# Turning attention's queries, keys and probabilities by VectorE's square blocks and device memory instead of TensorE transposes

## The chip, the cores and the metric

The kernel runs on one core of a Trainium2 chip. The metric is the device time of one execution in microseconds (us). The engines of the core run side by side and meet only at semaphores: TensorE (PE) multiplies matrices, VectorE (DVE), ScalarE (ACT) and GpSimd (POOL) work element by element, and SyncE (SP) issues nearly all transfers (DMA).

## What is computed

The reference is a block of two layers on 16 sequences of 64 tokens of width 512, all in float32. The part that matters here is the first one, a cross-attention with 32 query heads and 8 key heads:

```
kv = concatenate([context, latents], axis=1)             # 128 keys for each sequence
q = rms_norm(latents @ Wq)   per head, 32 heads of 128
k = rms_norm(kv @ Wk)        per head, 8 heads of 128;   v = kv @ Wv
scores = einsum('bhgqd,bhkd->bhgqk', q, k) * 128 ** -0.5
probs = softmax(scores);     out = (probs @ v) @ Wo
```

A feed-forward layer with 4-bit weights follows, then a second attention and a second feed-forward layer with low-rank additions. The change doesn't touch those three, but the 4-bit weights are unpacked (dequantized) by VectorE in the background of the first attention.

## The kernel before, in words

The first attention is cut into 64 units: 8 key heads times 8 pairs of sequences (`UNITS`). A unit has four query heads for two sequences of 64 tokens, so its queries are a tile of 128 tokens by 4 x 128 (`b_q`), its keys and values two tiles of 128 by 128 each (`b_kv`), its scores four tiles of 128 by 128 (`b_s`). Products that need float32 accuracy are three passes over a high and a low part (`HI`, `LO`; `PASSES`): ScalarE copies a value to its rounded high part, another engine subtracts to get the low part.

The work is software-pipelined by hand. Each engine has a function for one step `j` (`pe_step0`, `act_step0`, `dve_step0`, `pool_step0`), and in a step it treats several units at once, each in another phase: `st.has(lag, UNITS)` is the part for unit `j - lag`. Each engine runs its instructions strictly in the order in which the code writes them; a wait on a semaphore holds all that is behind it on that engine.

In a step TensorE does, in order: the query projection of unit `j` (12 matmuls, L354), the transposes of queries and keys of unit `j-1` (six, L380 and L383, from `qn` and `kn`), the key and value projection of `j` (24, L366), the scores of `j-1` (L394), the transposes of the probabilities of `j-2` (four, L406), the output product of `j-3` (12, L418) and the product of probabilities and values of `j-2` (6, L431).

The queries and keys need a normalization first: ScalarE squares (L527, L542), VectorE sums (L579, L589), GpSimd takes the power -1/2 (L671, L674), VectorE multiplies (L585, L609). The softmax is VectorE's maximum (L595), ScalarE's four exponentials, each with a sum (L553), VectorE's reciprocal and multiplication (L614, L616).

In the background of the steps: the next key head's weights are loaded (`weight_load`), rounded by ScalarE at the end of its step (`hi_piece`, L455 or L459), and their low part computed by GpSimd at the end of its step (`lo_piece`, L468 or L472). In steps 5 to 57, 35 chunks of 4-bit weights are unpacked in three VectorE operations each (`dequant`, L1062, L1066, L1069), two in a step, in two fixed places of VectorE's order (`dve_between`); their factors are gathered by GpSimd (`gather_row`, L849), the chunks loaded and stored by SyncE (L776, L785, L788).

## Time and profile before

| what | value |
|---|---|
| time, median of 3 runs | 1143.39 us (1141.55 to 1143.66) |
| the profiled execution's own time | 1142.94 us, of which the span of its instructions 1141.1 us |
| busy share of the span | TensorE 96%, VectorE 68%, ScalarE 46%, GpSimd 35% |
| granted TensorE clock | 0.99 of full speed, mean |
| transfers | 89.05 MB, 78 GB/s over the span |

The span is that of one execution recorded by the profiler; around it lie 1.8 us. The first attention takes the part of the span up to about 760 us. A step's length can be read from the start of the same matmul in two steps that follow each other: the scores (L394) of one begin at 400.10 us and of the next at 411.18 us, so a step takes 11.08 us.

### The profile page before, as it was taken

The page shows a single profiled execution, that of the slowest core. Times are in us where ns is not written, and L with a number is a line of the kernel's source. Part 1 is how long each engine was busy: PE and PEld are TensorE (multiplying, and loading weights), DVE is VectorE, ACT ScalarE, POOL GpSimd, SP SyncE. Part 2 cuts the span into 40 slices and gives each one's busy share as a digit, 9 for nine tenths or more (in the row PEclk, how much of TensorE's full clock was granted, in tenths as well). Part 3 has the DMA queues.
Part 4 walks back from the last instruction along what each step waited for, and adds up shares of the span by engine and source line. Part 5 has one row for each costly group of instructions (what it writes and reads, how often), then busy time and mean ns, then how long its engine had stood idle before and what let it go on. Part 6 is the DMA issues. An engine that isn't in the chain of part 4 may idle for free. (4 is left out here: it accounts for less than half of the span.)

```text
span 1141.1 us, 18735 instructions
## 1 busy us (share of the span) xinstructions
PE 1097.6 (96%) x6533; PEld 950.9 (83%) x6533; DVE 773.4 (68%) x1496; ACT 523.9 (46%) x1398; POOL 398.5 (35%) x385
## 2 busy tenths in 40 slices
PE   4899999999999999999999999999999999888998
PEld 3789899998989999898989989878877777677877
DVE  7577777777777777777777765764344566889863
ACT  4354544545455454544544444443223445465531
POOL 4443343433334343343434321210002334575521
PEclk7899999999999999999999999999999999999999
DMA  6322323332332323233232120022202244143300
GB/s 221 82 79 71 104 63 98 88 96 69 92 103 64 97 89 96 68 102 106 70 103 84 50 91 1 1 80 89 65 1 56 65 111 111 43 104 77 84 10 37
DMA packets 65376, 89.05 MB, mean 78 GB/s; under 512 B 15544, under 2 KB 35024, under 8 KB 65284
## 3 DMA queue, kind: packets, MB, share of 16 engines
q1 hardware_dynamic: 60788, 70.95, 22.0%
q0 software_dynamic: 4496, 16.91, 4.8%
q8 instruction: 53, 0.87, 0.3%
q14 instruction: 39, 0.32, 0.1%
HBM read 64.64 MB, written 10.74 MB: 66 GB/s over the span
## 5 line engine op out<-in xcount | busy, mean ns | idle before, releaser
L366 PE MATMUL bank<-wqkv,kvT 128*128 128x256 f32 x1536 | 199.9, 286 | 2.1 <-DVE vv L570 2.1
L418 PE MATMUL bank<-wo,aoT 128*128 128x512 f32 x768 | 191.8, 398 | 0.0
L366 PEld LDWEIGHTS bank<-wqkv,kvT 128*128 128x128 f32 x1536 | 187.9, 191 | 3.7 <-DVE vv L570 3.6
L354 PE MATMUL bank<-wqkv,kvT 128*128 128x512 f32 x768 | 189.1, 395 | 1.6 <-DVE qn L585 1.6
L354 PEld LDWEIGHTS bank<-wqkv,kvT 128*128 128x128 f32 x768 | 141.8, 191 | 28.9 <-issue 1.8
L418 PEld LDWEIGHTS bank<-wo,aoT 128*128 128x128 f32 x768 | 139.6, 188 | 27.2
L671 POOL TENSOR_TENSOR rms<-msq,half_neg 128x4 f32<-128x4 f32 x64 | 80.0, 1249 | 202.7 <-DVE msq L581 202.5
L527 ACT ACTIVATE qsq<-bank 128x512 f32<-128x512 f32 x64 | 38.2, 597 | 115.3 <-PE bank L354 115.3
L553 ACT ACTIVATE prob<-bank,nmax 128x128 f32<-128x128 f32 x256 | 90.1, 371 | 2.2 <-DVE nmax L595 2.2
L585 DVE TENSOR_TENSOR qn<-bank,rms 128x512 f32<-128x512 f32 x64 | 44.3, 692 | 61.0 <-POOL rms L671 61.0
L674 POOL TENSOR_TENSOR rms<-msq,half_neg 128x2 f32<-128x2 f32 x64 | 44.8, 699 | 116.5 <-DVE msq L591 116.5
L542 ACT ACTIVATE ksq<-bank 128x256 f32<-128x256 f32 x64 | 24.5, 383 | 125.8 <-PE bank L366 125.8
L903 PE MATMUL bank<-x2T,wgu 128*128 128x512 f32 (+1 forms) x336 | 81.0, 396 | 1.0 <-issue 0.6
L579 DVE TENSOR_REDUCE ssq<-qsq 128x4 f32<-128x512 f32 x64 | 44.0, 687 | 49.0 <-ACT qsq L527 48.2
L903 PEld LDWEIGHTS bank<-x2T,wgu 128*128 128x128 f32 (+1 forms) x336 | 62.2, 186 | 16.9 <-DVE wd L864 0.8
L1975 POOL TENSOR_TENSOR pr<-pr,rc 128x512 f32<-128x512 f32 x52 | 54.4, 1049 | 54.7 <-DVE rc L1839 54.6
L394 PE MATMUL bank<-kT,qT 128*128 128x128 f32 x512 | 67.6, 275 | 1.2 <-ACT qT L531 1.2
L514 ACT ACTIVATE aoT<-bank 128x512 fp32r<-128x512 f32 x64 | 38.3, 599 | 59.6 <-PE bank L431 59.6
L920 PE MATMUL bank<-wd,hT 128*128 128x512 f32 (+1 forms) x264 | 65.5, 395 | 0.0
L547 ACT ACTIVATE pT<-bank 128x512 fp32r<-128x512 f32 x64 | 38.2, 597 | 58.7 <-PE bank L406 58.7
L394 PEld LDWEIGHTS bank<-kT,qT 128*128 128x128 f32 x512 | 62.8, 192 | 1.4 <-ACT qT L531 1.4
L468 POOL TENSOR_TENSOR wqkv<-wqkv_raw,wqkv 128x768 fp32r<-128x768 f32 x28 | 51.6, 1844 | 31.4 <-ACT wqkv L455 31.1
(176 smaller groups left out, 2131.1 us busy)
## 6 DMA issues: line engine op xcount, KB each, us to landing
wqkv_raw<-in_L_xattn_Wq_dram SPq DMA_DIRECT2D x32, 256.0 KB, 2.6
wo_raw<-in_L_xattn_Wo_dram SPq DMA_DIRECT2D x32, 256.0 KB, 2.8
qS<-qhl SPq DMA_DIRECT2D x32, 256.0 KB, 3.8
wload<-w_gu SPq DMA_DIRECT2D x20, 256.0 KB, 3.2
w_gu<-qch SPq DMA_DIRECT2D x16, 256.0 KB, 2.3
kS<-chl SPq DMA_DIRECT2D x32, 128.0 KB, 3.1
qch<-_L_ffn_down_qweight_dram SPq DMA_DIRECT2D x10, 256.0 KB, 3.6
w_d<-qch SPq DMA_DIRECT2D x10, 256.0 KB, 2.0
```

The lines of the kernel that those rows point to most:

```text
L354: mm = pe.matmul(b_q[:, :], kvT[:, l, kt, p, 1:3, :], wqkv[:, par, r, kt, 0:QW], start=(kt == 0 and n == 0), stop=(kt == KT - 1 and n == 2))
L366: mm = pe.matmul(b_kv[:, b * 256:(b + 1) * 256], kvT[:, l, kt, p, 2 * b:2 * b + 2, :], wqkv[:, par, r, kt, QW:QKV], start=(kt == 0 and n = ...
L394: mm = pe.matmul(b_s[:, n * P:(n + 1) * P], qT[:, b, 2 * hp:2 * hp + 2, :], kT[:, b, :], start=True, stop=True)
L418: mm = pe.matmul(b_o[:, :], aoT[:, l, h, :, :], wo[:, par, r, h, :], start=(h == 0 and n == 0), stop=(h == G - 1 and n == 2))
L468: pool.tensor_tensor(wqkv[:, par, LO, n, :], wqkv_raw[:, n % 2, :], wqkv[:, par, HI, n, :].bitcast(F32), ALU.subtract).then_inc(s_wqkv, 1)
L553: act.activation(prob[:, n, :], b_s[:, n * P:(n + 1) * P], ACT.Exp, bias=nmax[:, n:n + 1], accum_out=psum_row[:, n:n + 1]).then_inc(s_exp, 1)
L585: dve.tensor_tensor(qn[:, :, :], b_q[:, :].rearrange("p (h d) -> p h d", h=G), rms[:, 0:4].unsqueeze(2).to_broadcast([P, G, HD]), ALU.mult ...
L671: pool.tensor_tensor(rms[:, 0:4], msq[:, 0:4], half_neg[:, 0:4], ALU.pow).then_inc(s_rq, 1)
L674: pool.tensor_tensor(rms[:, 4:6], msq[:, 4:6], half_neg[:, 4:6], ALU.pow).then_inc(s_rk, 1)
L903: mm = pe.matmul(b[0:w, :], wgu[:, f, l, m, kt, 0:w], x2T[:, r, kt, :], start=(kt == 0 and k == 0), stop=(kt == KT - 1 and k == 2))
L920: mm = pe.matmul(f_d[t][:, :], hT[0:w, l, t * P:(t + 1) * P], wd[0:w, f, r, :], start=(f == 0 and k == 0), stop=(f == FT - 1 and k == 2))
L1975: pool.tensor_tensor(of[:, to + t % KT, :], of[:, to + t % KT, :], rc1[:, t % 4:t % 4 + 1].to_broadcast([P, D]), ALU.mult).then_inc(s_n1, 1)
```

## The change

TensorE no longer transposes anything in these steps. A tile of 128 by 128 is turned in two halves. VectorE transposes it in square blocks of 32 by 32 (`dve.transpose`), after a multiplication that it did before too, which now writes to a PSUM bank (`b_n`) in an order of elements that suits the blocks. Then SyncE stores the result to device memory (`blocks_out`: 128 rows of 2 KB, for keys 1 KB) and loads it back in another order (`blocks_back`: each row of SBUF from four pieces of 512 bytes, for keys 256 bytes), which puts the blocks in their places. So each unit has six transfers more: queries, keys and probabilities, out and back.

With it come these: ScalarE sums the squares itself, in four plus two smaller operations, in place of VectorE's two sums; the key's scale is applied by ScalarE after the load; the probabilities' low part is subtracted by GpSimd from SBUF instead of by VectorE from PSUM; the values bank `b_kv` is doubled. The scores of unit `j-1` now stand at the end of TensorE's step, behind the output product, the maximum and the exponentials come a step later, and the product with the values is that of unit `j-3`, behind the query projection. In the tables: the load of the first three weight tiles of the feed-forward layer moves into steps 62 to 64.

```diff
+            def sp_step0(st):
+                if st.has(1, UNITS):
+                    sp.wait_ge(s_k_out, st.done(1, 16))
+                    wait(sp, s_s, st.done(2))
+                    blocks_back(sp, kT[:, :, :, :], k_turn).then_inc(s_k_back, 16)
+                if st.has(2, UNITS):
+                    sp.wait_ge(s_pB, st.done(2))
+                    wait(sp, s_p_back, st.done(3, 16))
+                    blocks_out(sp, p_turn, pB[:, :, :, :]).then_inc(s_p_out, 16)
+                if st.j >= 1:
+                    weight_load(st.j - 1)
+                sp_stores(sp, st.j)
...
+                if st.has(2, UNITS):
+                    sp.wait_ge(s_p_out, st.done(2, 16))
+                    wait(sp, s_pv, st.done(3))
+                    blocks_back(sp, pT[:, LO, :, :, :].bitcast(F32), p_turn).then_inc(s_p_back, 16)
+                if st.has(0, UNITS):
+                    sp.wait_ge(s_qB, st.done(0))
+                    wait(sp, s_q_back, st.done(1, 16))
+                    blocks_out(sp, q_turn, qB[:, :, :, :]).then_inc(s_q_out, 16)
+                sp_loads(sp, st.j)
+                if st.has(0, UNITS):
+                    sp.wait_ge(s_kB, st.done(0))
+                    wait(sp, s_k_back, st.done(1, 16))
+                    blocks_out(sp, k_turn, kB[:, :, :, :]).then_inc(s_k_out, 16)
+                    sp.wait_ge(s_q_out, st.done(0, 16))
+                    wait(sp, s_s, st.done(1))
+                    blocks_back(sp, qT[:, :, :, :], q_turn).then_inc(s_q_back, 16)
...
+        def blocks_out(sp, to, frm):
+            return sp.dma_start(to.rearrange("a p r -> (a p r)").rearrange("(p c) -> p c", p=P),
+                                frm.rearrange("p b h t -> p (b h t)"))
+
+        def blocks_back(sp, to, frm):
+            return sp.dma_start(to.rearrange("p a h t -> p a (h t)"), frm.rearrange("a p r -> p a r"))
...
         def act_step0(st):
             act = nc.scalar
+            if st.has(2, UNITS):
+                act.wait_ge(s_max, st.done(2))
...
+                    act.activation(prob[:, n, :], b_s[:, n * P:(n + 1) * P], ACT.Exp, bias=nmax[:, n:n + 1],
+                                   accum_out=psum_row[:, n:n + 1]).then_inc(s_exp, 1)
+            if st.has(0, UNITS):
+                act.wait_ge(s_q, st.done(0))
...
+                for h in range(G):
+                    act.activation(b_sq[:, h * HD:(h + 1) * HD], b_q[:, h * HD:(h + 1) * HD], ACT.Square,
+                                   accum_out=ssq[:, h:h + 1]).then_inc(s_qsq, 1)
...
             if st.has(2, UNITS):
-                act.wait_ge(s_pt, st.done(2))
+                act.wait_ge(s_p_back, st.done(2, 16))
                 wait(act, s_pv, st.done(3))
-                act.activation(pT[:, HI, :, :], b_pt[:, :].rearrange("p (b q) -> p b q", b=2), ACT.Copy).then_inc(s_phi, 1)
...
+                act.activation(pT[:, HI, :, :, :], pT[:, LO, :, :, :].bitcast(F32), ACT.Copy).then_inc(s_phi, 1)
             hi_piece(act, st)
 
         def dve_step0(st):
             dve = nc.vector
+            if st.has(2, UNITS):
+                dve.wait_ge(s_s, st.done(2))
+                wait(dve, s_exp, st.done(3, 4))
+                dve.tensor_reduce(nmax[:, :], b_s[:, :].rearrange("p (n k) -> p n k", n=4), AX, ALU.max,
+                                  negate=True).then_inc(s_max, 1)
+            dve_between(dve, st.j, "exp")
+            if st.has(2, UNITS):
+                dve.wait_ge(s_exp, st.done(2, 4))
+                dve.reciprocal(rsum[:, :], psum_row[:, :]).then_inc(s_rec, 1)
+                dve.wait_ge(s_rec, st.done(2))
+                dve.tensor_tensor(b_n[:, :].rearrange("p (b a k) -> p b a k", b=4, a=4),
+                                  prob[:, :, :].rearrange("p a (k b) -> p b a k", b=4),
+                                  rsum[:, :].unsqueeze(1).unsqueeze(3).to_broadcast([P, 4, 4, 32]),
+                                  ALU.mult).then_inc(s_pn, 1)
+                dve.wait_ge(s_pn, st.done(2))
+                wait(dve, s_p_out, st.done(3, 16))
+                dve.transpose(pB[:, :, :, :].rearrange("p b h t -> p (b h t)"), b_n[:, :]).then_inc(s_pB, 1)
...
+            if st.has(2, UNITS):
+                pool.wait_ge(s_phi, st.done(2))
+                pool.tensor_tensor(pT[:, LO, :, :, :], pT[:, LO, :, :, :].bitcast(F32), pT[:, HI, :, :, :].bitcast(F32),
+                                   ALU.subtract).then_inc(s_plo, 1)
             gather_row(pool, st.j)
             lo_piece(pool, st)
```

The two sets of rows that follow are TensorE's order in one step of the middle of the attention, before and after. `bank0` holds the queries, `bank4` the scores, `bank5` the turned probabilities, `bank6` the product with the values, `bank7` the output product.

```order
255 L354 MATMUL bank0<-wqkv,kvT 128x512 x12
256 L380 MATMUL bank2<-ident,qn 128x128 x4
257 L383 MATMUL bank3<-ident,kn 128x128 x2
258 L366 MATMUL bank1<-wqkv,kvT 128x256 x24
259 L394 MATMUL bank4<-kT,qT 128x128 x4
260 L406 MATMUL bank5<-ident,prob 128x128 x4
261 L418 MATMUL bank7<-wo,aoT 128x512 x12
```

```order
215 L400 MATMUL bank0<-wqkv,kvT 128x512 x12
216 L442 MATMUL bank6<-pT,vv 128x256 x6
217 L418 MATMUL bank1<-wqkv,kvT 128x256 x24
218 L465 MATMUL bank7<-wo,aoT 128x512 x12
219 L428 MATMUL bank4<-kT,qT 128x128 x4
```

The ten transposes (L380, L383, L406) are gone, the scores stand behind the output product, and the product with the values (L431 before, L442 after) stands behind the query projection.

SyncE's queue in the same part of the program, before and after: names with `_turn` are the tensors in device memory through which a tile is turned.

```order
129 L258 DMA wqkv_raw<-in_L0_xattn_Wq_dram 128x512
130 L259 DMA wqkv_raw<-in_L0_xattn_Wk_dram 128x128
131 L260 DMA wqkv_raw<-in_L0_xattn_Wv_dram 128x128
132 L788 DMA w_gu<-qch 128x4x128
133 L264 DMA wo_raw<-in_L0_xattn_Wo_dram 128x512
```

```order
251 L339 DMA p_turn<-pB 128x512
252 L265 DMA wqkv_raw<-in_L0_xattn_Wq_dram 128x512
253 L266 DMA wqkv_raw<-in_L0_xattn_Wk_dram 128x128
254 L267 DMA wqkv_raw<-in_L0_xattn_Wv_dram 128x128
255 L833 DMA w_gu<-qch 128x4x128
256 L343 DMA pT<-p_turn 128x4x128
257 L339 DMA q_turn<-qB 128x512
258 L821 DMA qch<-in_L0_ffn_up_qweight_dram 128x1x512
259 L339 DMA k_turn<-kB 128x256
260 L343 DMA qT<-q_turn 128x4x128
261 L343 DMA kT<-k_turn 128x4x64
```

The load of the turned probabilities (`pT<-p_turn`) stands behind up to five other issues: the three of a weight piece and the one or two of a store.

GpSimd's order in a step, before and after (`pT` is the low part of the probabilities, `wo` or `wqkv` the low part of a weight piece):

```order
138 L671 TENSOR_TENSOR rms<-msq,half_neg 128x4
139 L674 TENSOR_TENSOR rms<-msq,half_neg 128x2
140 L849 DMA rows<-table_up_1,idx 128x1024
141 L472 TENSOR_TENSOR wo<-wo_raw,wo 128x512
```

```order
153 L712 TENSOR_TENSOR rms<-msq,half_neg 128x4
154 L715 TENSOR_TENSOR rms<-msq,half_neg 128x2
155 L718 TENSOR_TENSOR pT<-pT 128x512
156 L904 DMA rows<-table_up_2,idx 128x704
157 L506 TENSOR_TENSOR wqkv<-wqkv_raw,wqkv 128x768
```

One operation of 512 elements is added, ahead of the gather and the weight piece.

## Rows read from the trace of the kernel before

**Rows 1.** Busy us (and instructions) of PE, PEld, DVE, ACT, POOL; clock, DMA share, GB/s.

```profile
88.42:675.66 587.24, 587.24 (x3807) 530.90 (x3806) 427.39 (x792) 286.71 (x847) 223.56 (x191) 1.00 0.27 84
737.21:759.97 22.76, 20.97 (x118) 17.77 (x117) 17.71 (x34) 12.56 (x28) 6.21 (x7) 1.00 0.11 35
```

**Rows 2.** Waits of TensorE, 60 to 700 us: total us, times, longest.

```profile
PE bank L366 <- DVE vv L570: 0.4, 1, 0.4
```

**Rows 3.** Timeline of TensorE, 404 to 416 us: start, length, engine, line.

```profile
404.90 2.91 PE L354 MATMUL bank<-wqkv,kvT 128*128 128x512 f32 x12
407.65 0.60 PE L380 MATMUL bank<-ident,qn 128*128 128x128 f32 x4
408.09 0.38 PE L383 MATMUL bank<-ident,kn 128*128 128x128 f32 x2
408.22 3.12 PE L366 MATMUL bank<-wqkv,kvT 128*128 128x256 f32 x24
411.18 1.06 PE L394 MATMUL bank<-kT,qT 128*128 128x128 f32 x8
412.07 0.60 PE L406 MATMUL bank<-ident,prob 128*128 128x128 f32 x4
412.43 3.00 PE L418 MATMUL bank<-wo,aoT 128*128 128x512 f32 x12
415.27 0.88 PE L431 MATMUL bank<-pT,vv 128*128 128x256 f32 x6
```

**Rows 4.** Timeline of the softmax and the work behind it, 402 to 406 us.

```profile
402.12 0.36 ACT L553 ACTIVATE prob<-bank,nmax 128x128 f32<-128x128 f32 x1
...
403.49 0.65 ACT L459 ACTIVATE wo<-wo_raw 128x512 fp32r<-128x512 f32 x1
403.65 0.18 DVE L614 RECIPROCAL rsum<-psum_row 128x4 f32<-128x4 f32 x1 [0.37 <-ACT prob L553]
403.87 0.69 DVE L616 TENSOR_TENSOR prob<-prob,rsum 128x512 f32<-128x512 f32 x1
...
404.23 1.48 POOL L472 TENSOR_TENSOR wo<-wo_raw,wo 128x512 fp32r<-128x512 f32 x1 [0.91 <-ACT wo L459]
404.48 1.52 DVE L1062 TENSOR_SCALAR qch<-qch,shift 128x512 int32<-128x512 int32 x1
```

**Rows 5.** DMA issues on the page: count, KB each, median us from issue to landing.

```profile
wo_raw<-in_L_xattn_Wo_dram SPq DMA_DIRECT2D x32, 256.0 KB, 2.8
...
wload<-w_gu SPq DMA_DIRECT2D x20, 256.0 KB, 3.2
w_gu<-qch SPq DMA_DIRECT2D x16, 256.0 KB, 2.3
...
w_d<-qch SPq DMA_DIRECT2D x10, 256.0 KB, 2.0
```

**Rows 6.** Landings of the store L788, 100 to 700 us.

```profile
DMA to landing us min/median/max: 1.9/2.3/4.0
```

**Rows 7.** One line's durations: ACT L455, DVE L1062 (ns min/median/max).

```profile
L455 ACT ACTIVATE wqkv<-wqkv_raw x28: 835/865/866, 39.5 to 636.8; 128x768 fp32r<-128x768 f32 x28
...
L1062 DVE TENSOR_SCALAR qch<-qch,shift x35: 397/487/2102, 87.3 to 653.7; 128x512 int32<-128x512 int32 x26, 128x352 int32<-128x352 int32 x8, 96x512 int32<-96x512 int32 x1
```

**Rows 8.** Timeline of SyncE's queue: start, length of the issue.

```profile
431.99 0.38 SPq L788 DMA_DIRECT2D w_gu<-qch  x1
```

**Rows 9.** DMA queue q1, 398.6:401.6 (L788 alone) and 498.7:502 (L785 alone): packets, MB, share.

```profile
q1 hardware_dynamic: 528, 0.26, 30.0%
...
q1 hardware_dynamic: 144, 0.26, 21.0%
```

**Rows 10.** Timeline, 409 to 411 us: GpSimd's power beside VectorE's unpacking.

```profile
409.28 0.69 DVE L1066 TENSOR_TENSOR qch<-qch,rows 128x512 f32<-128x512 int32 x1
409.45 1.42 POOL L671 TENSOR_TENSOR rms<-msq,half_neg 128x4 f32<-128x4 f32 x1 [3.74 <-DVE msq L581]
410.90 0.69 DVE L585 TENSOR_TENSOR qn<-bank,rms 128x512 f32<-128x512 f32 x1 [0.93 <-POOL rms L671]
```

273 lines of the change are left out of this document (127 added, 146 removed).

## The prediction

> **What bounds the kernel now.** I read the busy time by stretch first. Over 587 us, which are steps 5 to 57 of the attention (53 steps of 11.08 us), TensorE is busy in every microsecond at full clock, while VectorE is busy for 427 us, ScalarE 287 and GpSimd 224, and the transfers take 27% of the DMA engines [rows 1]. The list of waits agrees: in 640 us TensorE waited once, for 0.4 us [rows 2]. So in a step the length is the sum of what TensorE issues. The timeline divides it by the starts of its groups: query projection 2.75 us, transposes of queries and keys 0.57, key projection 2.96, scores 0.89, transposes of probabilities 0.36, output product 2.84, and the product with the values, up to the next step's start at 415.98 us (404.90 + 11.08), 0.71 [rows 3].
>
> **What goes from TensorE.** The ten transposes: 0.57 + 0.36 = 0.93 us of a step. If nothing else bound, a step would be 10.15 us, and 64 steps would save 60 us. The question is what the new paths allow in 10.15 us, since each engine holds its order.
>
> **The path of the probabilities.** It is a ring: the exponentials of one unit, their turning, the load, then on ScalarE the high part and a weight piece, and behind these the exponentials of the next unit. What can't run faster than this ring sets the step. From one start of the exponentials to the next:
> - exponentials up to the reciprocal: 403.65 - 402.12 = 1.53 us; reciprocal to multiplication 0.22; multiplication 0.69 + 0.04 for the semaphore [rows 4].
> - The block transpose of 512 elements: no row shows one. From below it is 0; from above I take twice an operation of that size, 1.4 us. I take 0.69, the duration of the multiplication of the same size, the nearest row [rows 4].
> - The store of 256 KB: 2.0 us for rows of 2 KB, 2.3 for pieces of 512 bytes [rows 5]. I take 2.15. The worst of that second kind took 4.0 [rows 6].
> - The load in pieces of 512 bytes: between 2.8 (rows of 2 KB) and 3.2 (from a tensor that was itself stored by this program) [rows 5]; I take 2.95. Three semaphores around the two transfers: 0.15.
> - High part from SBUF 0.65, like L459 [rows 4], less the 0.05 by which it overlaps its successor; weight piece 0.65 or 0.87 in turn [rows 4, 7], mean 0.76, of which I count 0.74.
>
> Sum: 1.53 + 0.22 + 0.73 + 0.69 + 2.15 + 2.95 + 0.15 + 0.60 + 0.74 = 9.76 us. That is under 10.15, with 0.4 us of room. Two things use more than the room.
>
> *Issue and queueing.* Between store and load SyncE issues a weight piece and, in 35 of 53 steps, a store of unpacked weights, up to five issues of about 0.4 us [rows 8], 2.0 us behind the 0.4 of the store itself, so that the load can be issued a few tenths late; and their 256 to 640 KB lie in the queue ahead of the load. A 256 KB store in 512-byte pieces fills all engines for 0.30 x 3.0 = 0.90 us, one in 2 KB rows for 0.21 x 3.3 = 0.69 [rows 9]. The six new transfers are 1.25 MB in a step and by these prices 4.0 to 4.5 us of all DMA engines, so their share goes from 27% to about 67%. I put queueing at 0.45 us of the ring, between 0 (all falls into gaps) and 1.6 (the store at 3.0, the load at 3.7).
>
> *VectorE and GpSimd.* The rows show that these two stop each other on operands in SBUF: the unpacking L1062 takes 0.49 us as a rule but up to 2.10 [rows 7]; in the timeline it took 1.52 where it began 0.25 us after GpSimd's L472, and ended 0.29 us after that did [rows 4]. The other way round GpSimd's power took 1.42 us where it began beside an unpacking [rows 10]. Before, the multiplication L616 mostly ran while GpSimd was idle. Now GpSimd subtracts the low part of 512 elements (1.48, like L472) just as ScalarE goes on to the weight piece, then issues a gather, then does its own weight piece (1.48 to 1.84); that lies over the time 0.7 to 3.5 us behind the start of the exponentials, and the multiplication stands at 1.75. A stall is between 0 and 1.2 us; I take 0.6.
>
> The Trainium skill has this rule on its page SBUF — State Buffer, section Who interferes with whom: a VectorE instruction with two SBUF inputs and a GpSimd instruction that reads SBUF exclude each other, and who starts first keeps the port for the whole instruction. The trace agrees for the unpacking; no row shows it for L616. By that rule alone, with GpSimd always first, the stall would be 1.2 us in each step.
>
> So the ring is 9.76 + 0.45 + 0.6 = 10.8 us in steps 5 to 57.
>
> **VectorE's own ring.** The transposes (512, 512, 256 elements) replace two sums (512, 256) and the low part of 512, so its busy time stays 427.39 / 587.24 x 11.08 = 8.06 us. But it now waits through the exponentials (1.7 us from the maximum's end, with one unpacking of about 0.6 inside them), and for the two powers, of which the first alone cost it 0.93 us before [rows 10]; now the low parts of output and values, about 1.0 us, lie beside the first and an unpacking beside the second, so I take 0.6 for both. That is 8.06 - 0.6 + 1.7 + 0.6 = 9.8 us, 10.4 with the stall of 0.6: close behind the ring of the probabilities. ScalarE, 286.71 / 587.24 x 11.08 = 5.4 us busy, gets about 0.5 us more and has room.
>
> What hides the rest: the queries' round trip of about 5.3 us starts some 7.5 us into a step and is needed 9.3 us into the next; that of the keys starts 2 us later and its load is scaled by ScalarE about 5 us into the next step. Without this cover each would cost its whole 5.3 us.
>
> **The sum.** Steps 5 to 57: 53 x (10.8 - 11.08) = -15 us. The other 11 steps have no unpacking: about -0.93 each, less for the first ones, which fill the pipeline, and the last, which have the next layer's statistics on VectorE: -7. The end: before, from 737.21 us, 22.76 us were left to the last output product, and TensorE was busy for 20.97 of them [rows 1]. After, two units' exponentials must pass the ring one behind the other: 9.8, then 3.2 + 5.3 + 0.6 to the second one's high part, 1.5 for its low part, then values, their parts and the output product, 0.7 + 1.5 + 2.9, and 1 ahead of it: 26.5, so +4. The start I leave at nothing; its one more round trip is behind the second query projection. -15 - 7 + 4 = -18 us. The profiled execution took 1142.94 us, 0.45 under the median of the runs shown; so 1125 us.
>
> **Rivals.**
> - *All is hidden.* If the stall and queueing fall in the 0.4 us of room, TensorE bounds again: 64 x -0.93 + 4 = -56, so 1087 us. For it: both terms are zero from below, and the sum has 0.4 us. Against: the DMA share of 67%, and GpSimd's new operation stands just there.
> - *The round trip is too long (slower).* The place is the wait of ScalarE for the probabilities' load. Without its trip the ring is 9.76 - 5.25 = 4.5 us, 5.1 with the stall, so it passes 11.08 when store and load together take over 6.0 us, where I forecast 5.7. With the store at 2.6, the load at 3.7 and 0.3 of late issue, it is 6.6, the step 11.7: 53 x 0.62 - 3 = +30, so 1173 us. For it: store maxima of 4.0 [rows 6] at 27% share, and the share more than doubles.
> - *VectorE's new operations are dear.* With block transposes at twice the row's price its ring is 10.4 + 0.69 + 0.69 + 0.41 = 12.2 us: 53 x 1.1 + 4 = +62, some 1205 us. The Trainium skill, page Advanced Engine Details and Errata, section SBUF Cachelines, speaks for it: reads that touch another 16-byte line each time pay a penalty, and the multiplication now reads every fourth float32. No run here shows such a read.
>
> **Numbers.** Forecast as above (1100 to 1141 us) 0.39; all hidden 0.19; round trip too long 0.28; dear operations 0.08; a step within a few hundredths of 11.08, no change, 0.06. Faster by over 0.2%, which is about what a measurement of this kernel tells from none, is 0.58, slower 0.36. The range reaches from the first rival to the middle of the second: 1086 to 1176 us.
>
> **What would show it.** Right: scores of two steps 10.8 us apart; TensorE idle a few tenths in a step, ended by ScalarE's or VectorE's low part of the output, by the low part of the probabilities or by `qn`; ScalarE idle ahead of the high part (L591), ended by the DMA; the multiplication L606 often over 0.69 us. STREAM_TRANSPOSE at about 0.69, stores at 2.0 to 2.4, loads at 2.8 to 3.3. Wrong: landings over 3.5 us, or a transpose over 1 us (slower), or TensorE without idle time and 10.15 us steps (all hidden).

## The result, and the profile after

The changed kernel takes 1220.26 us (median of 4 runs, 1217.82 to 1222.04) beside 1142.71 for the kernel before (4 runs in the same session): a ratio of 1.0673, interval 1.0653 to 1.0693, so 77.5 us slower. The forecast was 1125 us, the range 1086 to 1176. The profiled execution took 1221.74 us, 78.8 more than that of before.

The busy time of the stretch that answers to [rows 1], 52 spacings of the multiplication L606 (steps 5 to 57), in the same columns, and under it that of the drain of the attention:

```profile
92.64:722.27 629.63, 545.80 (x3214) 467.07 (x3213) 456.33 (x780) 289.13 (x1296) 289.44 (x242) 1.00 0.62 187
760.00:840.00 80.00, 60.10 (x300) 50.69 (x298) 43.30 (x89) 29.06 (x108) 20.44 (x22) 0.87 0.34 108
```

A step takes 629.63 / 52 = 12.11 us in place of 11.08, and TensorE, which was never idle, is busy for 87% of it. No other engine is over 73%. No engine is full, so what sets the step is a chain of waits. The list of TensorE's waits, 87 to 690 us, against the one wait of 0.4 us in [rows 2]:

```profile
PE bank L442 <- POOL pT L718: 41.9, 45, 3.2
PE bank L465 <- DVE aoT L622: 35.1, 34, 1.5
PE bank L465 <- issue: 6.8, 6, 1.6
```

The page's costliest groups and its DMA issues say where the chain is: ScalarE is idle for 319 us ahead of the high part of the probabilities L591, always for the load, and the multiplication takes 2131 ns on average where [rows 4] had 0.69 us.

```profile
L591 ACT ACTIVATE pT<-pT 128x512 fp32r<-128x512 f32 x64 | 40.5, 632 | 319.3 <-DMA pT<-p_turn 319.3
L606 DVE TENSOR_TENSOR bank<-prob,rsum 128x512 f32<-128x512 f32 x64 | 136.4, 2131 | 2.2
...
q_turn<-qB SPq DMA_DIRECT2D x64, 256.0 KB, 4.0
...
p_turn<-pB SPq DMA_DIRECT2D x64, 256.0 KB, 2.0
pT<-p_turn SPq DMA_DIRECT2D x64, 256.0 KB, 3.9
```

One turn of the ring in the timeline, from the first exponential of a unit (L554) to that of the next, which answers to [rows 4]:

```profile
406.54 0.35 ACT L554 ACTIVATE prob<-bank,nmax 128x128 f32<-128x128 f32 x1
...
407.40 1.02 POOL L904 DMA_INDIRECT rows<-table_up,idx  x1 [0.17 <-issue]
...
408.06 0.18 DVE L604 RECIPROCAL rsum<-psum_row 128x4 f32<-128x4 f32 x1 [3.21 <-ACT prob L554]
408.27 2.94 DVE L606 TENSOR_TENSOR bank<-prob,rsum 128x512 f32<-128x512 f32 x1
408.46 1.86 POOL L506 TENSOR_TENSOR wqkv<-wqkv_raw,wqkv 128x768 fp32r<-128x768 f32 x1
411.24 0.72 DVE L612 STREAM_TRANSPOSE pB<-bank 128x512 f32<-128x512 f32 x1
411.99 0.33 SPq L339 DMA_DIRECT2D p_turn<-pB  x1
...
414.05 0.38 SPq L343 DMA_DIRECT2D pT<-p_turn  x1
...
418.08 0.63 ACT L591 ACTIVATE pT<-pT 128x512 fp32r<-128x512 f32 x1 [6.19 <-DMA pT<-p_turn]
...
419.14 0.35 ACT L554 ACTIVATE prob<-bank,nmax 128x128 f32<-128x128 f32 x1
```

The multiplication began at 408.27 and ended at 411.21, 0.89 us after GpSimd's weight piece L506 (410.32), although the piece began 0.19 us later than it did. Of the 50 multiplications between 90 and 700 us in the trace, 49 end 0.88 to 0.91 us after the piece beside them: they are 1.32 to 1.77 us long in the 17 where the piece stands alone and had begun 0.4 to 1.1 us earlier, and 2.60 to 3.37 in the 32 where a gather stands ahead of the piece, which then begins 0.18 to 0.62 us later than they do.

Where the time was lost can be read from the starts of the output products (L418 before, L465 after):

| output product of unit | before | after | later by |
|---|---|---|---|
| 2 | 90.41 | 96.14 | 5.7 |
| 56 | 690.06 | 745.97 | 55.9 |
| 60 | 734.38 | 789.65 | 55.3 |
| 63 | 757.08 | 834.42 | 77.3 |
| end of the span | 1141.1 | 1219.9 | 78.8 |

So 50 us are the steps, 22 the last three units, 6 the start, and what follows the attention costs 1.5. The four units from 56 to 60 win only 0.6: three of these steps take 10.0 to 10.1 us, the fourth 13.6.

### The profile page after: what moved, and what is told of

It is laid out like the page before. It is cut to its first block and busy times, and to the rows that moved or that the text cites. A ratio compares the mean times of both kernels' runs of the same rounds, so it can differ in the third digit from the quotient of the medians.

```text
span 1219.9 us, 18668 instructions
## 1 busy us (share of the span) xinstructions
PE 1065.9 (87%) x5893; PEld 893.0 (73%) x5893; DVE 810.7 (66%) x1496; ACT 535.9 (44%) x1974; POOL 478.7 (39%) x449
## 5 line engine op out<-in xcount | busy, mean ns | idle before, releaser
L465 PE MATMUL bank<-wo,aoT 128*128 128x512 f32 x768 | 193.7, 401 | 53.5 <-DVE aoT L622 46.7
L465 PEld LDWEIGHTS bank<-wo,aoT 128*128 128x128 f32 x768 | 141.2, 190 | 90.4 <-DVE aoT L622 54.3
L418 PE MATMUL bank<-wqkv,kvT 128*128 128x256 f32 x1536 | 198.8, 287 | 0.0
L400 PE MATMUL bank<-wqkv,kvT 128*128 128x512 f32 x768 | 195.2, 403 | 1.7 <-DVE bank L631 1.7
L418 PEld LDWEIGHTS bank<-wqkv,kvT 128*128 128x128 f32 x1536 | 193.2, 196 | 0.2
L591 ACT ACTIVATE pT<-pT 128x512 fp32r<-128x512 f32 x64 | 40.5, 632 | 319.3 <-DMA pT<-p_turn 319.3
L718 POOL TENSOR_TENSOR pT<-pT 128x512 fp32r<-128x512 f32 x64 | 84.4, 1319 | 204.1 <-ACT pT L591 204.1
L606 DVE TENSOR_TENSOR bank<-prob,rsum 128x512 f32<-128x512 f32 x64 | 136.4, 2131 | 2.2
L712 POOL TENSOR_TENSOR rms<-msq,half_neg 128x4 f32<-128x4 f32 x64 | 65.6, 1025 | 116.0 <-DVE msq L619 115.7
L442 PE MATMUL bank<-pT,vv 128*128 128x256 f32 x384 | 62.9, 300 | 54.7 <-POOL pT L718 54.5
L442 PEld LDWEIGHTS bank<-pT,vv 128*128 128x128 f32 x384 | 50.4, 191 | 79.2 <-POOL pT L718 78.8
L604 DVE RECIPROCAL rsum<-psum_row 128x4 f32<-128x4 f32 x64 | 11.4, 178 | 141.7 <-ACT prob L554 141.7
L715 POOL TENSOR_TENSOR rms<-msq,half_neg 128x2 f32<-128x2 f32 x64 | 59.2, 924 | 110.3 <-DVE msq L640 110.3
L554 ACT ACTIVATE prob<-bank,nmax 128x128 f32<-128x128 f32 x256 | 89.6, 360 | 7.7 <-DVE nmax L599 7.7
L562 ACT ACTIVATE bank<-bank 128x128 f32<-128x128 f32 x256 | 70.9, 277 | 2.1 <-PE bank L400 2.1
```

The source lines that it names most:

```text
L400: mm = pe.matmul(b_q[:, :], kvT[:, l, kt, p, 1:3, :], wqkv[:, par, r, kt, 0:QW], start=(kt == 0 and n == 0), stop=(kt == KT - 1 and n == 2))
L418: mm = pe.matmul(kv_bank(st, 0)[:, b * 256:(b + 1) * 256], kvT[:, l, kt, p, 2 * b:2 * b + 2, :], wqkv[:, par, r, kt, QW:QKV], start=(kt == ...
L442: mm = pe.matmul(b_pv[:, b * 256:(b + 1) * 256], vv[:, par, l, b, :], pT[:, r, :, b, :], start=(n == 0), stop=(n == 2))
L465: mm = pe.matmul(b_o[:, :], aoT[:, l, h, :, :], wo[:, par, r, h, :], start=(h == 0 and n == 0), stop=(h == G - 1 and n == 2))
L554: act.activation(prob[:, n, :], b_s[:, n * P:(n + 1) * P], ACT.Exp, bias=nmax[:, n:n + 1], accum_out=psum_row[:, n:n + 1]).then_inc(s_exp, 1)
L562: act.activation(b_sq[:, h * HD:(h + 1) * HD], b_q[:, h * HD:(h + 1) * HD], ACT.Square, accum_out=ssq[:, h:h + 1]).then_inc(s_qsq, 1)
```

## The experiments

Each time stands beside runs of the kernel before in its own session. For the ring I read the same five stretches out of each timeline, as means over 52 turns (units 3 to 55, which are steps 5 to 57); they add up to the spacing of the multiplications. The forecast's row has its terms in the same stretches (0.73 + 0.6; 0.69; 2.15 + 0.10; 2.95 + 0.45 + 0.05; 0.60 + 0.74 + 1.53 + 0.22). "Rest" is conversion L591 to the next multiplication: conversion, weight piece, exponentials, reciprocal.

| kernel | time, us | step | multiply | its end to store issue | store issue to load issue | load issue to conversion | rest |
|---|---|---|---|---|---|---|---|
| forecast | 1125 | 10.8 | 1.33 | 0.69 | 2.25 | 3.45 | 3.09 |
| changed | 1220.3 | 12.11 | 2.35 | 0.78 | 2.25 | 3.84 | 2.89 |
| e1 prob in PSUM | 1163.4 | 11.10 | 0.70 | 0.78 | 3.05 | 3.69 | 2.89 |
| e2 read in a row | 1202.3 | 11.76 | 2.00 | 0.78 | 2.30 | 3.81 | 2.89 |
| e3 load first | 1267.0 | 13.03 | 2.54 | 2.06 | 2.35 | 3.19 | 2.90 |
| e5 queue | 1208.1 | 11.93 | 2.46 | 0.79 | 2.53 | 3.25 | 2.91 |
| e6 rows of 2 KB | 1203.0 | 11.79 | 2.33 | 0.78 | 2.24 | 3.54 | 2.89 |
| e11 e1 and e5 | 1200.0 | 11.64 | 0.70 | 0.89 | 3.89 | 3.23 | 2.93 |
| e12 GpSimd later | 1299.4 | 13.56 | 1.10 | 0.78 | 4.75 | 4.04 | 2.88 |
| e13 e12, loads later | 1238.9 | 12.48 | 1.10 | 0.78 | 2.24 | 5.38 | 2.98 |
| e15 piece later | 1176.5 | 11.26 | 1.11 | 0.78 | 2.80 | 3.68 | 2.88 |

**e1: the exponentials kept in PSUM.**

```diff
-                    act.activation(prob[:, n, :], b_s[:, n * P:(n + 1) * P], ACT.Exp, ...
+                    act.activation(b_s[:, n * P:(n + 1) * P], b_s[:, n * P:(n + 1) * P], ACT.Exp, ...
-                                  prob[:, :, :].rearrange("p a (k b) -> p b a k", b=4),
+                                  b_s[:, :].rearrange("p (a k b) -> p b a k", a=4, b=4),
```

> Exponentials are written over the scores in PSUM bank 4, and the multiply behind the reciprocal reads them there, so that it has no large operand in SBUF; the next scores wait for the multiply. Exclusion theory (the multiply is held up by GpSimd's elementwise operations and gather over SBUF, and its 2.6 us set the ring): the multiply falls to 0.70 to 1.1 us with or without GpSimd at work, the spacing of the multiplies in steps 5 to 57 falls from 12.1 us to 10.4 to 10.8, the kernel to 1140 to 1160 us. Rival (the transfers set the ring; VectorE's delay only fills time in which the load would be waited for): the multiply shortens, but the load lands later or is waited for longer, the spacing stays above 11.7, the kernel above 1195 us.

1163.44 us, ratio 1.0173 (1.0151 to 1.0195). All multiplications take the same time (ns, min/median/max):

```profile
L606 DVE TENSOR_TENSOR bank<-bank,rsum x64: 698/699/700, 56.5 to 768.7; 128x512 f32<-128x512 f32 x64
```

The spacing, 11.10 us, misses the exclusion theory's window of 10.4 to 10.8, and so does the time by 3 us, since of the 1.65 us won 0.80 come back in the store:

```profile
409.33 0.37 SPq L343 DMA_DIRECT2D kT<-k_turn  x1
411.52 0.33 SPq L339 DMA_DIRECT2D p_turn<-pB  x1
```

The keys' load is now issued 2.2 us ahead of the store of the probabilities, where it was 4.7 in the changed kernel (407.31 and 411.99); the store takes 3.0 us in the median, not 2.0. That this load is what makes it longer is a reading of the timeline and not shown: in 18 turns of e1 the load was issued 3 to 4 us ahead, and the store took 3.2 us there too. The rival is out, since it had the spacing above 11.7.

**e2: the same multiplication, reading one float32 after another.** Its probabilities end up in another order, so the output isn't the reference's; sizes and counts are the same.

```diff
-                                  prob[:, :, :].rearrange("p a (k b) -> p b a k", b=4),
+                                  prob[:, :, :].rearrange("p a (b k) -> p b a k", b=4),
```

> The multiply reads the probabilities one float32 after another, not every fourth: same count, same result tile, the elements stand in another order (the attention output is that of a permuted key order). If the strided read has a price of its own of 0.4 us (1.09 against 0.69 us alone) and the rest is GpSimd's exclusion: 0.70 us where GpSimd is idle, still 2.2 to 2.9 us beside its operations, the kernel 1200 to 1216 us. Rival (the strided read is what makes it 2.6 us): the median falls below 1.2 us, the kernel to 1140 to 1160 us.

1202.31 us, ratio 1.0518 (1.0494 to 1.0542). The shortest one takes 0.70 us against 1.07, the median 2.27 against 2.61:

```profile
L606 DVE TENSOR_TENSOR bank<-prob,rsum x64: 699/2271/2946, 58.2 to 800.3; 128x512 f32<-128x512 f32 x64
```

So reading every fourth float32 costs 0.35 to 0.4 us, and the rest of the excess isn't the stride. Shortest, median and time are the first theory's.

**e3 and e5: SyncE's order.** e3 puts weight loads and the stores and tile loads of the feed-forward weights behind the load of the probabilities and the store of the queries.

```diff
-                if st.j >= 1:
-                    weight_load(st.j - 1)
-                sp_stores(sp, st.j)
...
                     blocks_out(sp, q_turn, qB[:, :, :, :]).then_inc(s_q_out, 16)
+                if st.j >= 1:
+                    weight_load(st.j - 1)
+                sp_stores(sp, st.j)
```

> In each step SP issues the load of the turned probabilities and the store of the queries ahead of the weight loads, the w_gu and w_d stores and the tile loads, which before stood between the store and the load of the probabilities. If the load's 4.0 us (3.2 in the quiet steps 58 to 61) come from standing behind those transfers: the landing falls to 3.2 to 3.4 us, the step by 0.6 to 0.7, the kernel to 1180 to 1190 us. Rival (it shares the rings with whatever runs at the time, 63% busy): the landing stays at 3.8 to 4.1, the kernel within 8 us of 1220.

1266.96 us, ratio 1.1078 (1.1058 to 1.1098): 47 us slower than the changed kernel, which neither theory had. The load did land in 3.2 us, but SyncE's queue shows what was put behind what:

```profile
416.43 0.43 SPq L833 DMA_DIRECT2D w_gu<-qch  x1
420.14 0.55 SPq L821 DMA_DIRECT2D qch<-in_L_ffn_up_qweight_dram  x1
420.79 0.53 SPq L339 DMA_DIRECT2D k_turn<-kB  x1
```

The load of quantized rows waits for the landing of the store issued at 416.43, and the keys' store stands behind it: 8.9 us after the store of the probabilities (411.91), where in the changed kernel it was 4.6 us (411.99 and 416.63). e5 gives that load to the next step, behind the keys' load, and puts the weight transfers behind the keys' store.

```diff
+                if st.j >= 1:
+                    sp_loads(sp, st.j - 1)
                 if st.has(2, UNITS):
                     sp.wait_ge(s_pB, st.done(2))
...
                     blocks_out(sp, k_turn, kB[:, :, :, :]).then_inc(s_k_out, 16)
+                if st.j >= 1:
+                    weight_load(st.j - 1)
+                sp_stores(sp, st.j)
```

> SP's order changed without the fault of the run before: the weight loads and the w_gu and w_d stores stand behind the store of the keys, and the loads of quantized rows, which wait for those stores, go to the next step behind the load of the keys. Nothing but turning transfers is issued between the store and the load of the probabilities. Queue theory: that load lands in 3.2 to 3.4 us as in the run before, nothing is held behind the quantized load, the step falls by 0.5 to 0.8 us to 11.3 to 11.6, the kernel to 1180 to 1195 us. Rival (the rings' total load makes the 4.0 us, and the last run's 3.2 us was only its longer step): the landing stays at 3.7 to 4.0, the kernel 1205 to 1225 us.

1208.11 us, ratio 1.0569 (1.0551 to 1.0586). The load's share fell by 0.6 us as the queue theory said, and 0.3 of it came back in the store, since keys and queries are now loaded later and lie beside it. The step fell by 0.18, so the gain is the rival's, though its reason isn't.

**e6: the load in rows of 2 KB**, in place of pieces of 512 bytes. The probabilities end up in the wrong places, so the output isn't the reference's; the bytes are the same.

```diff
-                    blocks_back(sp, pT[:, LO, :, :, :].bitcast(F32), p_turn).then_inc(s_p_back, 16)
+                    rows_back(sp, pT[:, LO, :, :, :].bitcast(F32), p_turn).then_inc(s_p_back, 16)
```

> The load of the turned probabilities fetches one row of 2 KB for each partition in place of four pieces of 512 bytes (the same 256 KB, elements in the wrong places, so the output is of mixed probabilities). If the pieces are what makes the load slower than the store (4.0 against 2.0 us): it lands in 2.0 to 2.6 us, the step falls by 1.4 to 1.9 until another ring or TensorE sets it, the kernel 1130 to 1150 us. Rival (it is the other transfers in flight): 3.5 to 4.0 us, the kernel above 1195 us.

1202.97 us, ratio 1.0529 (1.0512 to 1.0547): the rival's window. The piece size is worth 0.3 us of the load, the transfers issued ahead of it 0.6 (e5). The changed kernel shows the second by itself: from the load's issue to the conversion it is 3.3 us in the median of the 18 turns with no store of unpacked weights between store and load, 4.1 in the 34 with one.

**e12, e13, e15: GpSimd's order**, operands as in the changed kernel. e12 moves gather and weight piece one step later, behind the power of the queries.

```diff
                 pool.tensor_tensor(rms[:, 0:4], msq[:, 0:4], half_neg[:, 0:4], ALU.pow).then_inc(s_rq, 1)
+            if st.j >= 1:
+                gather_row(pool, st.j - 1)
+                lo_piece(pool, Step(0, st.j - 1))
...
-            gather_row(pool, st.j)
-            lo_piece(pool, st)
```

> The changed kernel with one thing moved: GpSimd's gather and its weight piece, which ran beside the multiply, stand one step later behind the power of the queries, when the multiply and the block transpose behind it are over; operands and their places in memory are as in the changed kernel. Exclusion theory (the multiply waits out GpSimd's operations): it takes 1.1 to 1.5 us (its own price, and what is left of GpSimd's low part of the probabilities), the spacing in steps 5 to 57 falls to 10.8 to 11.3 us, the kernel to 1150 to 1180 us. Rival (reading every fourth float32 from SBUF is slow whenever DMA and other engines are at work, and GpSimd only looks like the cause): it stays above 2 us, the kernel above 1205 us.

1299.43 us, ratio 1.1357 (1.1337 to 1.1377). The multiplication takes 1.10 us, the exclusion theory's number, and yet the kernel is the slowest of all. The store's row tells why:

```profile
414.65 0.33 SPq L339 DMA_DIRECT2D p_turn<-pB  x1
418.30 0.34 SPq L271 DMA_DIRECT2D wo_raw<-in_L_xattn_Wo_dram  x1
418.74 0.53 SPq L343 DMA_DIRECT2D pT<-p_turn  x1
```

The weight load waits until GpSimd's piece has freed its buffer, and the load of the probabilities stands behind it in the queue. e13 issues the weight loads a step later as well (`weight_load(st.j - 2)`).

> The changed kernel with GpSimd's gather and weight piece one step later, behind the power of the queries, and SP's weight loads one step later as well, so that they find their buffer free and nothing waits in SP's queue. Exclusion theory: the multiply takes 1.1 us as in the last such run, 1.5 us less than in the changed kernel, the store 2.0 and the load 4.0 us as there, the spacing 10.6 to 11.3 us, the kernel 1145 to 1180 us. Rival (the exclusion only moves to another of VectorE's operations on the ring, as to the powers or the keys' multiply): the multiply is short but the spacing stays at 11.8 us or more, the kernel above 1200 us.

1238.85 us, ratio 1.0837 (1.0809 to 1.0865), step 12.48: in the rival's window, but not for the rival's reason. Now it is the load that takes 5.4 us on average, beside the gather's transfers:

```profile
407.82 0.45 SPq L343 DMA_DIRECT2D pT<-p_turn  x1
...
411.85 0.63 ACT L591 ACTIVATE pT<-pT 128x512 fp32r<-128x512 f32 x1 [3.11 <-DMA pT<-p_turn]
...
418.02 1.02 POOL L906 DMA_INDIRECT rows<-table_up,idx  x1 [0.17 <-issue]
...
418.98 0.37 SPq L343 DMA_DIRECT2D pT<-p_turn  x1
...
424.40 0.63 ACT L591 ACTIVATE pT<-pT 128x512 fp32r<-128x512 f32 x1 [5.01 <-DMA pT<-p_turn]
```

Median from issue to conversion over the 52 turns: 6.2 us in the 34 with a gather issued within 2 us of it, 4.0 in the 18 without. All of those 18 have a store of unpacked weights ahead of the load; of the 34, the 16 that have one too take 6.5, the others 5.5. e15 leaves the gather in its place and moves only the piece (and the weight loads).

```diff
+            if st.j >= 1:
+                lo_piece(pool, Step(0, st.j - 1))
             if st.has(0, UNITS):
                 pool.wait_ge(s_kms, st.done(0))
...
             gather_row(pool, st.j)
-            lo_piece(pool, st)
```

> The changed kernel with GpSimd's weight piece alone one step later, behind the power of the queries, and the weight loads a step later; the gather stays where it is, over before the load of the probabilities is issued. If a multiply that begins beside GpSimd's work waits for the operations that GpSimd has next in hand: with nothing behind the gather it takes 1.1 to 1.6 us instead of 2.6, store and load stay at 2.0 and 4.0 us, the spacing in steps 5 to 57 falls by the 1.0 to 1.5 us that the multiply loses, to 10.6 to 11.1 us, the kernel to 1145 to 1170 us. Rival (transfers take it back, as in each run so far): the spacing stays above 11.6 us, the kernel above 1195 us.

1176.54 us, ratio 1.0295 (1.0278 to 1.0312). The multiplication is 1.1 us throughout, in the 34 cases beside a gather too:

```profile
L606 DVE TENSOR_TENSOR bank<-prob,rsum x64: 1076/1104/1123, 56.4 to 773.1; 128x512 f32<-128x512 f32 x64
```

So it is the piece that holds it. Of 1.24 us won, 0.85 stay; the store takes 0.55 more, as in e1. The time and the step (11.26 us) lie between the two theories' windows, next to the exclusion's.

**e11: e1 and e5 together.**

> Both cures of the changed kernel's ring at once: exponentials kept in PSUM (multiply 0.70 us) and nothing issued between the store and the load of the probabilities. If the step of 12.1 us is the sum of the ring's parts, then 1.9 us (multiply) and 0.8 us (load 4.0 to 3.2) come off, less up to 0.6 us where the keys' load still lies beside the store: 10.0 to 10.4 us for the step, where TensorE takes over, the kernel 1105 to 1130 us. Rival (what is taken off the multiply comes back in the transfers, as in the run with PSUM alone, where the store went from 2.0 to 3.1 us): 10.8 to 11.1 us, the kernel 1145 to 1160 us.

1200.01 us, ratio 1.0472 (1.0436 to 1.0509), 37 us slower than e1 alone and above both windows. The two cures don't add: with both, it is 3.9 us from the store of the probabilities to the load's issue, 3.05 in e1. By the timeline the store now lies beside the loads of queries and keys; that this is the cause is not shown.

**e4: the end.** The two layer norms of the step after the last unit go behind the low parts of output and values.

```diff
-            if st.j == UNITS:
-                ln_apply(dve, X2, 2, xn2[:, 2, :])
-                ln_apply(dve, X2, 3, xn2[:, 3, :])
...
                                   vv[:, par, HI, :, :].bitcast(F32), ALU.subtract).then_inc(s_vlo, 1)
+            if st.j == UNITS:
+                ln_apply(dve, X2, 2, xn2[:, 2, :])
+                ln_apply(dve, X2, 3, xn2[:, 3, :])
```

> In the first step after the last unit, VectorE's two applications of the layer norm (tiles 2 and 3) stand behind the low parts of the attention output and of the values, as they did in the kernel before, not ahead. Theory (8.3 us of VectorE idle there hold the output product of unit 61 and the 12 matmuls behind it): 6 to 10 us off the end, the kernel 1210 to 1214 us. Rival (the wait moves to the transposes of those tiles): within 3 us of 1220.

1214.44 us, ratio 1.0628 (1.0605 to 1.0651): 5.8 us off, just short of the 6 to 10. In the changed kernel the second of them waited for a power that stands on GpSimd behind the low part of the probabilities, and the output product behind that:

```profile
805.86 1.26 POOL L718 TENSOR_TENSOR pT<-pT 128x512 fp32r<-128x512 f32 x1 [9.54 <-ACT pT L591]
807.08 0.56 POOL L736 TENSOR_TENSOR rstd<-mv,half_neg 128x1 f32<-128x1 f32 x1
...
807.68 1.48 DVE L740 TENSOR_SCALAR xn<-acc,mv,rstd 128x512 f32<-128x512 f32 x1 [8.28 <-POOL rstd L736]
...
809.81 5.49 PE L465 MATMUL bank<-wo,aoT 128*128 128x512 f32 x12 [8.18 <-DVE aoT L622]
```

Of the 8.2 us 3.4 came back as a wait for the transposes of those tiles. From the output product of unit 60 to that of 63 it takes 39.8 us here and 44.8 in the changed kernel, 22.7 before.

**e7 and e10: one part undone.** e7 turns the probabilities on TensorE again; queries and keys go through memory. e10 is e7 with e4's edit.

```diff
+            if st.has(2, UNITS):
+                pe.wait_ge(s_pn, st.done(2))
+                wait(pe, s_plo, st.done(3))
+                for n in range(4):
+                    mm = pe.transpose(b_pt[:, n * P:(n + 1) * P], prob[:, n, :], ident[:, :])
+                mm.then_inc(s_pt, 1)
...
-                    blocks_out(sp, p_turn, pB[:, :, :, :]).then_inc(s_p_out, 16)
...
-                    blocks_back(sp, pT[:, LO, :, :, :].bitcast(F32), p_turn).then_inc(s_p_back, 16)
```

> One part undone: the probabilities are turned by TensorE again, four transposes behind the key projection, evicted by ScalarE and VectorE as in the kernel before; queries and keys go by square blocks and memory as in the changed kernel. Ring theory (the round trip of the probabilities through memory, between two groups of exponentials, is what makes the step 12.1 us): TensorE sets the step at 10.0 us of the quiet steps and 0.37 us for four transposes, 10.4 to 10.6 us, the kernel 1125 to 1140 us, below the kernel before. Rival (VectorE's work or the queries' and keys' round trips set it nearly as much): the step stays above 11.1 us and the kernel is slower than before.

> Probabilities turned by TensorE, queries and keys through memory, and the layer norm of the end behind the low parts. The first gives 1118 us by its own run; the second gave 6 us on the changed kernel, where the low part waited 8 us for it, and that wait is short here: 1112 to 1118 us, a ratio to the kernel before of 0.973 to 0.979. Rival: the end waits for something else in this kernel and nothing comes off, 1117 to 1119 us.

1118.02 us, ratio 0.9790 (0.9774 to 0.9806), and 1117.26 us, ratio 0.9774 (0.9758 to 0.9790): so they beat the kernel before by 24 and 26 us. The two intervals overlap, so e4's edit shows nothing here. The ring theory's step is met; its time was forecast 7 us too high. The busy time in e7's steps 5 to 57 is that of a kernel bound by TensorE, 543.77 / 52 = 10.46 us a step:

```profile
86.72:630.49 543.77, 543.77 (x3433) 490.37 (x3432) 380.63 (x781) 290.54 (x1299) 217.07 (x188) 1.00 0.55 167
```

**e8: the ring opened, nothing undone.** ScalarE converts the turned probabilities behind the next unit's exponentials; GpSimd's low part goes ahead of its powers, the scores ahead of the output product, the residual's addition a step later.

```diff
             if st.has(2, UNITS):
                 act.wait_ge(s_max, st.done(2))
...
+            if st.has(3, UNITS):
+                act.wait_ge(s_p_back, st.done(3, 16))
+                wait(act, s_pv, st.done(4))
+                act.activation(pT[:, HI, :, :, :], pT[:, LO, :, :, :].bitcast(F32), ACT.Copy).then_inc(s_phi, 1)
```

> All three still turn by blocks and memory, with the multiply as it is, but ScalarE's conversion of the turned probabilities stands behind the next unit's exponentials, not ahead, so that the round trip need not fit between them; GpSimd's low part stands ahead of its powers, the scores ahead of the output product, and the addition to the residual a step later. Ring theory: the load is no longer waited for, the step falls to 10.2 to 10.9 us (TensorE, or VectorE's own work with the slow multiply), the kernel 1120 to 1155 us. Rival (bandwidth or VectorE's total work sets the 12.1 us): the step stays above 11.6 us, the kernel above 1190 us.

1187.65 us, ratio 1.0404 (1.0377 to 1.0431), the step 11.28 us: between the two windows. Of the 264 us that ScalarE waited for the load in 600 us of the changed kernel, nothing is left among the longest waits. But another chain, all on engines, takes its place, and it lasts in the quiet steps too, those from 58 on that unpack nothing (11.0 to 12.0 us): the maximum stands on VectorE behind the keys' multiplication, and exponentials, conversion, low part and the values' product follow it.

```profile
409.06 0.65 DVE L599 TENSOR_REDUCE nmax<-bank 128x4 f32<-128x512 f32 x1
...
409.75 0.37 ACT L554 ACTIVATE prob<-bank,nmax 128x128 f32<-128x128 f32 x1 [2.20 <-DVE nmax L599]
...
411.86 1.79 POOL L711 TENSOR_TENSOR pT<-pT 128x512 fp32r<-128x512 f32 x1 [1.86 <-ACT pT L559]
...
413.70 0.98 PE L442 MATMUL bank<-pT,vv 128*128 128x256 f32 x6 [0.99 <-POOL pT L711]
```

**e9, e16, e14: the opened ring, tuned.** e9 is e8 with the exponentials in PSUM (e1), the maximum ahead of the keys' multiplication, and e4's edit. e16 adds e15's edit, e14 adds e5's order.

```diff
             dve_between(dve, st.j, "rk")
+            if st.has(1, UNITS):
+                dve.wait_ge(s_s, st.done(1))
+                wait(dve, s_exp, st.done(2, 4))
+                dve.tensor_reduce(nmax[:, :], b_s[:, :].rearrange("p (n k) -> p n k", n=4), AX, ALU.max,
+                                  negate=True).then_inc(s_max, 1)
```

> All three operands still turned through memory, with the exponentials in PSUM, ScalarE's conversion of the turned probabilities behind the next exponentials, the maximum ahead of the keys' multiply, scores ahead of the output product and the layer norm of the end moved back. If only rings held the changed kernel, TensorE's 10.0 us are left, 10.0 to 10.5 us a step, the kernel 1090 to 1125 us, below the kernel before. Rival (transfers at a step of 10 us are over 75% busy and land late: keys at 4.3 us in the last such run): the scores wait for keys or queries, 10.8 us or more, the kernel above 1150 us.

> The version with all rings opened (1137 us, 10.85 us a step) with GpSimd's weight piece a step later, behind the power of the queries. If exclusion of VectorE (up to 3.7 us on one dequantization) delays its store of the keys: 10.2 to 10.6 us a step, the kernel 1100 to 1125 us. Rival (the keys' 4.5 us store and the transfers' total set it): 10.8 us or more, 1133 us or more.

> The version with all rings opened (1137 us) with SP's order of the queue run: weight loads and w_gu and w_d stores behind the keys' store, loads of quantized rows behind the keys' load. If the keys' late load (store 4.5 us behind other transfers) is a matter of order: the step falls from 10.85 to 10.0 to 10.4 us, the kernel 1095 to 1120 us. Rival (the transfers' total, some 75% of the rings at that step, or the queue's waits, as in the run with PSUM and queue, where the store of the probabilities took 3.5 us): 10.8 us or more, the kernel 1135 us or more.

e9: 1136.93 us, ratio 0.9951 (0.9927 to 0.9974), step 10.85. e16: 1134.33, ratio 0.9904 (0.9867 to 0.9941), step 10.80. e14: 1191.4, ratio 1.0406 (1.0375 to 1.0436), step 11.72. All three met their rivals' steps and not the first theories'; e9's time lies between its two windows. With all three operands turned through memory the kernel is thus at best 0.5 to 1% faster than before. In e9 the scores wait for the keys, whose load is issued 4.5 us behind their store, 3.0 in the changed kernel; freeing VectorE (e16) gave next to nothing, and e5's order made it worse. In e9's quiet steps the output products stand 9.97 us apart: there, without the unpacking and its transfers, TensorE sets the step. Whether a better order of the queue or only fewer bytes would reach 10.0 us in the other steps stays open.

## Why the prediction was wrong, point by point

**TensorE without the transposes: right.** In steps 58 to 60 of the changed kernel, which unpack nothing, the multiplications stand 10.00 us apart, and TensorE is busy all the time; forecast was 10.15.

```profile
732.29 1.28 DVE L606 TENSOR_TENSOR bank<-prob,rsum 128x512 f32<-128x512 f32 x1
...
742.29 1.10 DVE L606 TENSOR_TENSOR bank<-prob,rsum 128x512 f32<-128x512 f32 x1
```

**The ring of the probabilities sets the step: right.** e7 takes its trip through memory out and the step is TensorE's; e8 opens it and the wait for the load is gone. A mistake in the place would have shown there.

**The terms of the ring: its length was 1.3 us more than forecast** (12.11 against 10.8, first two lines of the table). By terms:
- *"A stall is between 0 and 1.2 us; I take 0.6."* This step failed most. The multiplication takes 2.35 us on average, 1.62 over the 0.73 that I gave it, 1.02 over that with the stall. Two causes lie in it, told apart by experiments: its own price of 0.35 to 0.4 us for every fourth float32 (e2), and 1.24 us for GpSimd's weight piece (e15). The second is the upper end of my bound and not its middle: GpSimd's operations stand back to back just there, and the piece, which began after the multiplication in 32 of 49 cases, still finished first. By the rule of the Trainium skill, page SBUF — State Buffer, section Who interferes with whom, the prediction came to 1.2 us in each step, near the 1.24 measured, but with GpSimd always first, which it was in 17 of 49; so the agreement is in part luck. Nor do these rows bear out the second half of the rule, that the first keeps the port: in the 32 the multiplication began first and still waited. The page speaks of the order of issue, and the rows have starts, so why it lost stays open. The row by which the prediction found the rule borne out (L1062) doesn't fit its clause on two inputs in SBUF: it is a TENSOR_SCALAR that reads one tile and one column of shifts.
- *Queueing of 0.45 us and a load of 2.95:* store issue to conversion is 6.09 us against 5.70, and all of it lies in the load (3.84 against 3.45). The prediction's own sign of being wrong, landings over 3.5 us, was met by the load's 3.9. By e6 and e5, 0.3 us of the load are its pieces and 0.6 what is issued ahead of it.
- *Conversion, weight piece, exponentials:* 2.89 against 3.09, in my favour. From the multiplication's end to the store's issue it is 0.78 against 0.69, the block transpose and its semaphore.

The block transpose at 0.72 us (forecast 0.69) and the 62% DMA share (67%) were right.

**The end: +4 forecast, +22 measured.** I let two units pass the ring one after the other, but held each at TensorE's pace beside it. In the last three steps TensorE has no projections and needs 7.8, 8.7 and 6.3 us; a ring that no longer fits in 11 us costs its whole length there: 20.2, 13.0 and 11.6 us between output products. The layer norm that stands behind it is 5 of the 22 (e4).

Another part is TensorE's clock, which the prediction left out of the end. Over 760 to 840 us the mean granted clock is 0.87, against 1.00 in the same part of the kernel before [rows 1]. The longest stretch at the lower level, 1.2 GHz, holds the output product of unit 61, behind 8.2 us without a matmul; its 12 matmuls took 5.49 us, 2.91 for those of unit 60 at the full level:

```profile
789.65:792.56 2.91, 2.91 (x16) 2.42 (x15) 1.05 (x3) 0.63 (x4) 0.70 (x1) 1.00 0.95 330
809.81:815.30 5.49, 5.49 (x13) 4.27 (x14) 1.47 (x3) 0.00 (x0) 0.48 (x1) 0.50 0.00 0
```

That is 2.6 us of the 13.0 from this product to that of unit 62; how much of the 22 the clock makes in all, no run shows. Start: +6 where I had nothing, and no run looks into it.

**The sum.** 53 steps at 10.8 gave -15 us, 53 at 12.11 give +55 (the table's 50 counts two quiet steps in). Of the -7 for the other steps little came: the gain of the quiet steps, some 1 us each, is lost again in the 13.6 us from the output product of unit 59 to that of unit 60. The end took 18 more than forecast, the start 6. The second rival (round trip too long, over 6.0 us for store and load) was met at 6.09 us, but its 1173 us counted the stall at 0.6; the third rival's strided read was real, at a fifth of the 1.79 us that made its 1205. The three don't exclude each other in one ring: their excesses add, and I priced each with the others at their middle. That is why the range ended at 1176.

**What each excess was worth by itself.** In e1, e15 and e5 between a third and 70% of what one part of the ring gave up came back in another, in the transfers each time. By the timelines each edit moves stores and loads of the three operands against each other; which of them lengthens which, no run separates.

## What to carry to other kernels

A round trip through memory belongs on a path only where another unit's work can lie beside it. Before a transpose is taken off a full TensorE, walk the ring of waits that replaces it and add all its uncertain terms at once, and price the last steps of the loop, where the ring stands alone. Here the four transposes of the probabilities are worth their 0.46 us of TensorE (10.46 us a step in e7, 10.00 without them), and the six of queries and keys are not: turning only those through memory is the 2% gain.

In an in-order DMA queue a transfer that waits is a wall: moving one there cost 0.9 us a step in e3 and 1.45 in e12, 47 and 79 us in all, although both had shortened the part of the ring that they were made for.

## What the runs showed of the hardware

- A VectorE multiplication over SBUF ended 0.88 to 0.91 us behind a GpSimd subtraction over SBUF in 49 of 50 cases, whichever had begun first: in 32 the subtraction began 0.18 to 0.62 us after it. In the one case where that was 0.94 us, the multiplication took 1.10 us, undisturbed. A gather issued by GpSimd (1.02 us on its engine) didn't lengthen it at all in 34 cases (1.09 to 1.12 us). With its large operand in PSUM it took 0.70 us whatever GpSimd did.
- Freed from one operation, the exclusion finds the next: in e9 an unpacking (`L1118`, 128x352) that takes 0.39 us where it runs undisturbed took 3.68 beside three GpSimd operations in a row, and ended 0.22 us after the last:

```profile
407.55 1.03 POOL L904 DMA_INDIRECT rows<-table_up,idx  x1 [0.18 <-issue]
...
408.24 3.68 DVE L1118 TENSOR_SCALAR qch<-qch,shift 128x352 int32<-128x352 int32 x1
...
408.61 1.86 POOL L506 TENSOR_TENSOR wqkv<-wqkv_raw,wqkv 128x768 fp32r<-128x768 f32 x1
...
410.40 1.30 POOL L711 TENSOR_TENSOR pT<-pT 128x512 fp32r<-128x512 f32 x1
```

- A 512-element multiplication from SBUF took 1.07 us at its shortest when it read every fourth float32 and 0.70 when it read them in a row; from PSUM every fourth cost nothing (0.70).
- A load of 256 KB took 3.3 us to its user with only a weight piece issued ahead of it, 4.1 with a store of unpacked weights too (both in the changed kernel), and 6.5 with a gather's transfers beside it as well (e13).
